# Attention kernel: the next group's filters prepared from step 20 of the last superblock but one, with the spatial filter's products spread among other matmuls

## What is computed

```python
x = x + ddf(gn(x))        # decoupled dynamic filter: 3x3 taps, channel filter times spatial filter
x = x + v * att           # 1x1 products, one sigmoid gate per pixel
x = x + conv3x3(gn(x))    # ternary weights
x = x + attention(gn(x))  # 3136 queries and 3136 keys per image, dk 16, dv 64
```

```python
y  = relu(pooled @ w1.T + b1) @ w2.T + b2            # channel filter, 64 x 9, then centred and scaled
sf = einsum('bchw,nc->bnhw', xn, ws) + bs            # spatial filter, 9 values per pixel
sf = (sf - sf.mean(2)) / (sf.std(2, ddof=1) + 1e-10) # centred and scaled over the 9
```

## Time and profile before

| | us |
|---|---|
| median of 3 runs | 1804.92 |
| lowest and highest | 1804.43, 1806.83 |
| the profiled execution | 1803.89 |
| span of its instructions | 1802.0 |
| TensorE's mean granted clock in it | 0.965 |
| PE, DVE, ACT, POOL busy | 91%, 69%, 67%, 61% of the span |

### The profile page before, as it was taken

How to read it: one execution, slowest core, us unless ns; L and a number is a source line. 1 busy time by engine, 2 the same in 40 slices (tenths; PEclk the granted TensorE clock), 3 DMA queues, 4 the chain that set the end, 5 groups by cost and what they waited for, 6 DMA issues and landing times.

```text
span 1802.0 us, 35669 instructions
## 1 busy us (share of the span) xinstructions
PE 1643.3 (91%) x10892; PEld 835.9 (46%) x10892; DVE 1240.5 (69%) x2443; ACT 1212.8 (67%) x2300; POOL 1101.6 (61%) x926
## 2 busy tenths in 40 slices
PE   5987899999889799999988879999998788999997
PEld 4364444444436345444444634444443364444442
DVE  5946777775584777777367478777738648877760
ACT  2045889998403689999731278999972237899995
POOL 2720488789551058888955106888887402688888
PEclk9989999999989899999988899999999899999999
DMA  2004000000000400000000040000000002000000
GB/s 87 0 1 90 2 7 7 7 7 11 8 0 1 90 2 7 7 7 7 12 8 0 1 90 2 7 7 11 8 7 6 0 20 35 2 12 6 7 7 11
DMA packets 12423, 27.16 MB, mean 15 GB/s; under 512 B 4560, under 2 KB 8912, under 8 KB 11728
## 3 DMA queue, kind: packets, MB, share of 16 engines
q1 hardware_dynamic: 12240, 24.92, 5.9%
HBM read 8.73 MB, written 6.42 MB: 8 GB/s over the span
## 4 chain that ended last, share of the span: by engine, by line
PE 59%; issue 15%; POOL 10%; DVE 9%; ACT 6%; POOLq 1%; DVEq 0%; ACTq 0%
PE PS L1315 26%; PE PS L1271 12%; PE PS L1241 12%; DVE nmt L688 4%; ACT Pb L956 2%; POOL VT L1024 2%; POOL VT L1029 2%; POOL VT L1026 2%; PE PS L1213 2%; DVE nmt L681 2%; POOL VT L1033 2%; ACT PS L911 1%; PE PS L1204 1%; POOL accP L1076 1%; PE PS L1205 1%
## 5 line engine op out<-in xcount | busy, mean ns | idle before, releaser
L681 DVE TENSOR_REDUCE nmt<-PS 128x1 f32<-128x448 f32 x1176 | 681.6, 618 | 211.0 <-PE PS L1241 208.0
L1076 POOL TENSOR_TENSOR accP<-accP,Pb 128x512 f32<-128x512 f32 (+1 forms) x532 | 676.7, 1272 | 125.9 <-ACT Pb L956 97.5
L956 ACT ACTIVATE Pb<-PS 128x896 f32<-128x896 f32 (+1 forms) x700 | 637.5, 915 | 128.5 <-PE PS L1271 118.9
L1315 PE MATMUL PS<-Pb,VT 128*64 128x448 f32 x2800 | 659.9, 544 | 4.8 <-ACT Pb L956 4.1
L1241 PE MATMUL PS<-Ka,Qa 96*64 96x448 bf16 x2888 | 499.8, 358 | 23.6 <-ACT PS L911 10.7
L1271 PE MATMUL PS<-Qa,Ka 99*64 99x448 bf16 x2744 | 491.7, 353 | 3.3 <-ACT Pb L956 2.8
L911 ACT ACTIVATE PS<-PS,nmt 128x448 f32<-128x448 f32 x588 | 356.6, 606 | 30.6 <-DVE nmt L688 28.6
L1241 PEld LDWEIGHTS PS<-Ka,Qa 96*64 96x64 bf16 x2888 | 168.3, 110 | 270.9 <-issue 117.6
L1271 PEld LDWEIGHTS PS<-Qa,Ka 99*64 99x64 bf16 x2744 | 168.4, 110 | 241.8 <-issue 187.4
L1315 PEld LDWEIGHTS PS<-Pb,VT 128*64 128x64 f32 x2800 | 194.9, 137 | 102.6 <-ACT Pb L956 30.3
L834 ACT ACTIVATE xnp<-xw,nb,rstd 128x448 f32<-128x448 f32 x56 | 40.5, 750 | 204.5 <-DVE nb L503 204.5
(11 more groups left out here) (145 smaller groups left out, 1478.4 us busy)
## 6 DMA issues: line engine op xcount, KB each, us to landing
xin<-in_x SPq DMA_DIRECT2D x4, 1568.0 KB, 11.9
out<-xw SPq DMA_DIRECT2D x28, 224.0 KB, 1.9
Qa<-parts SPq DMA_DIRECT2D x24, 168.0 KB, 7.6
Ka<-parts SPq DMA_DIRECT2D x24, 112.0 KB, 3.8
Ka<-parts SPq DMA_DIRECT2D x24, 84.0 KB, 2.6
Qa<-mpt SPq DMA_DIRECT2D x96, 1.3 KB
wz<-in_weights SPq DMA_DIRECT2D x1, 829.0 KB, 8.2
Qa<-parts SPq DMA_DIRECT2D x24, 28.0 KB, 1.9
```

The source lines that it names most:

```text
L681: nc.vector.reduce_max(nmt[:, target % 2, b, t:t + 1], PS[0:BLK, bank, 0:CH], X, negate=True).then_inc(mx_free, 1)
L956: nc.scalar.activation(Pb[0:r, j % PSLOTS, :, :], PS[0:r, 2 * (k % 2):2 * (k % 2) + 2, 0:CH], ACT.Exp).then_inc(exp_done, 1)
L1076: nc.gpsimd.tensor_tensor((accQ if j < TO_ACCP else accP)[0:r, :, REST:CH], (accQ if j <= TO_ACCP else accP)[0:r, :, REST:CH], Pb[0:r, j % ...
L1315: last = mm(PS[C * h:C * h + C, OB, 0:CH], VT[:, j, C * h:C * h + C], Pb[:, j % PSLOTS, h, :], start=(j == 0), stop=(j == NQ - 1))
```

## The change

The preparation keeps its operations and their number. What moves, in steps of superblock 5 and 6 (5/20 is superblock 5, step 20):

| operation | before | after |
|---|---|---|
| DVE `front_stats` | 6/0 | 5/19 (the same place in DVE's order) |
| PE `pair_mean`, `pair_var` | 6/2, 6/3 | 5/20, 5/21 |
| DVE `squares`, `var_eps`, `front_bias` | 6/3, 6/4, 6/6 | 5/20, 5/20, 5/23 |
| POOL `power` | 6/5 | 5/22 |
| ACT `front_normalise` | 6/7 to 6/13 | 5/24, 6/1 to 6/6 |
| PE spatial filter products | 6/8 to 6/14 | 6/2 to 6/8 |
| PE `front_mid` | 6/7 | 6/0 |
| DVE `front_sum_squares` | 6/15 | 6/8 |
| ACT `front_root` | 6/16 | 6/11 |
| PE `front_channel_filter` | 6/16 | 6/12 |
| DVE `front_parts`, `front_centre` | 6/18, 6/19 | 6/12, 6/15 |
| PE transposes | 20, 20, 21, 22, 23, 24, 24 | 16 to 22, one a step |
| POOL `channel_root` | 6/21 | 6/20 |

The four products of a step no longer stand together behind the scores: one stands between the values and the first pair of scores, one between the two pairs, two behind the second pair. The core of the diff:

```diff
-FRONT_XN = 7
-FRONT_SF = 8
-FRONT_TR = (20, 20, 21, 22, 23, 24, 24)
-FRONT_ROOT = 16
+SPLIT_STEP = 17
+FRONT_STATS = SPLIT_STEP + 2
+FRONT_MEAN = 20
+FRONT_XN = (24, 26, 27, 28, 29, 30, 31)
+FRONT_SF = FRONT_XN[0] + 3
+FRONT_SQUARES = 8
+FRONT_ROOT = 11
+FRONT_Y = 12
+FRONT_CENTRE = 15
+FRONT_TR = (16, 17, 18, 19, 20, 21, 22)
+FRONT_CF = 20
...
-            def front_spatial_filter(g, j):
-
-                pe.wait_ge(xn_ready[0], NJ * g + j + 1)
-                for i in range(4 * j, 4 * j + 4):
-                    last = mm(PS[0:SP2, SFB, i * PART:(i + 1) * PART], xnp[:, (2 * i + 1) * PW + 1:(2 * i + 3) * PW + 1],
-                              wcol("ws"), start=True, stop=True)
-                if j == NJ - 1:
+            def filter_rows(g, i):
+
+                if i % 4 == 0:
+                    pe.wait_ge(xn_ready[0], NJ * g + i // 4 + 1)
+                last = mm(PS[0:SP2, SFB, i * PART:(i + 1) * PART], xnp[:, (2 * i + 1) * PW + 1:(2 * i + 3) * PW + 1],
+                          wcol("ws"), start=True, stop=True)
+                if i == NSP - 1:
                     last.then_inc(sfT_ready, 1)
...
-                    if j == 2:
+                    if j == FRONT_MEAN:
                         pair_mean(g + 1, 0, front)
-                    elif j == 3:
+                    elif j == FRONT_MEAN + 1:
                         pair_var(g + 1, 0, front)
-                    elif j == 7:
+                    elif j == NQ:
                         front_mid(g + 1)
-                    elif j == 16:
+                    elif j == NQ + FRONT_Y:
                         pe.wait_ge(recip, NJ * g + NJ)
                         front_channel_filter(g + 1)
...
+                def filter_at(s, j, place):
+
+                    i = NQ * (s - NJ + 2) + j - FRONT_SF
+                    if more and s >= NJ - 2 and 0 <= i < NJ:
+                        for r in ((0,), (1,), (2, 3))[place]:
+                            filter_rows(g + 1, 4 * i + r)
...
                         if j:
                             values(j)
+                        filter_at(s, j, 0)
                         for h in range(2):
                             if j < NQ - 2 or s < NJ - 1:
...
                                 scores(k + 2, s + (j >= NQ - 2), h)
+                            filter_at(s, j, 1 + h)
                             if tiles:
                                 max_tile(*tiles.pop(0))
...
-                        if s == NJ - 1 and more:
-                            front_at(j)
+                        if s >= NJ - 2 and more:
+                            front_at(NQ * (s - NJ + 2) + j)
```

More of the change, by code:

```diff
@@ L937, in front_at @@
                 def front_at(j):
-                    if FRONT_XN <= j < FRONT_XN + NJ:
-                        front_normalise(g + 1, j - FRONT_XN)
-                    for i in range(NJ):
-                        if FRONT_TR[i] == j - 1:
-                            front_spatial_filter(g + 1, i)
-                    if j == FRONT_ROOT:
+                    if j in FRONT_XN:
+                        front_normalise(g + 1, FRONT_XN.index(j))
+                    if j - NQ - 1 in FRONT_TR:
+                        front_spatial_filter(g + 1, FRONT_TR.index(j - NQ - 1))
+                    if j == NQ + FRONT_ROOT:
                         front_root(g + 1)
@@ L982, in group @@
                     superblock(s)
-                if more:
-                    for j in range(NJ):
-                        if FRONT_TR[j] == NQ - 1:
-                            front_spatial_filter(g + 1, j)
                 copy_output(NJ * g + NJ - 1)
@@ L1056, in scale_sums, with superblock @@
                     nc.gpsimd.tensor_tensor(sme[:, :, :], sm[:, s % 2, :, :], ef[:, :, :], ALU.mult).then_inc(dstep, 1)
-                def superblock(sidx, s, first, front=False):
+                def superblock(sidx, s, first):
                     for j in range(1, NQ):
@@ L1061, in superblock @@
                             scale_sums(sidx, s)
-                        if front and j == 5:
+                        if more and s == NJ - 2 and j == FRONT_MEAN + 2:
                             power(g + 1, 0)
-                        if front and j == 21:
+                        if more and s == NJ - 1 and j == FRONT_CF:
                             channel_root(g + 1)
@@ L1084, in group @@
                     superblock(NJ * g + s, s, False)
-                superblock(NJ * g + NJ - 1, NJ - 1, False, more)
+                superblock(NJ * g + NJ - 1, NJ - 1, False)
                 finish(NJ * g + NJ - 1, NJ - 1)
@@ L1288, in front_at @@
                 def front_at(j):
-                    if j == 2:
+                    if j == FRONT_MEAN:
                         pair_mean(g + 1, 0, front)
-                    elif j == 3:
+                    elif j == FRONT_MEAN + 1:
                         pair_var(g + 1, 0, front)
-                    elif j == 7:
+                    elif j == NQ:
                         front_mid(g + 1)
-                    elif j == 16:
+                    elif j == NQ + FRONT_Y:
                         pe.wait_ge(recip, NJ * g + NJ)
                         front_channel_filter(g + 1)
-                    if FRONT_SF <= j < FRONT_SF + NJ:
-                        front_spatial_filter(g + 1, j - FRONT_SF)
-                    for i in range(NJ):
-                        if FRONT_TR[i] == j:
-                            front_transpose(g + 1, i)
+                    if j - NQ in FRONT_TR:
+                        front_transpose(g + 1, FRONT_TR.index(j - NQ))
+                def filter_at(s, j, place):
[3 more added lines that the diff above has]
+                            filter_rows(g + 1, 4 * i + r)
                 def superblock(s):
@@ L1379, in _ @@
             front_mid(0)
-            for j in range(NJ):
-                front_spatial_filter(0, j)
+            for i in range(NSP):
+                filter_rows(0, i)
             front_channel_filter(0)
```

19 lines of the change are left out of this document (8 added, 11 removed).

## The result

The changed kernel takes **1846.07 us** (median of 4 runs, 1845.15 to 1846.84) where the kernel before took 1804.87 on the same chip (1804.43 to 1806.83). The ratio is 1.0224, with a 95% interval of 1.0211 to 1.0237. It is slower, as forecast, but by 41 us and not by 21: the time lies 12 us above the upper end of the range.

A forecast was written before the change was run, and what follows sets the result against it. PE, busy 91% of the span, was taken to bound the kernel. Terms 2.8 + 3.6 + 1.0 = 7.4 us in groups 0 and 2, 6.5 in group 1, total 21.3, gave 1826 us; 8-in-10 range 1806 to 1834.

The forecast's parts named there:

- The mean's wait, 2.80 us: Superblock 5, step 20: PE waits 2.80 us for DVE's statistics ahead of the mean's matmul; +2.8 us a group.
- The spread, 3.6 us a group: Superblock 6, steps 2 to 8: products in three places each pay two switches, 0.51 us more a step; +3.6 us a group.
- B: Rival: spreading the products costs nothing more, as a switch is cheap without a semaphore wait before it; 1815 us, chance 0.20.
- E: Rival: one of each product's two weight loads is hidden; 1807 us, chance 0.10.
- F: Rival: the products' weight loads are all taken ahead and PE's steps fall to POOL's pace; 1799 us, chance 0.07.
- D: Rival: the stall for the mean is absorbed or doesn't occur; 1818 us, chance 0.06.
- the row of one matmul between half-array ones: Trace of the kernel before: a step with one small full-array matmul takes 1.59 us for 1.13, so 0.46 a matmul.
- Root and channel filter, +1.0 us: Superblock 6: +1.8 for the root's wait, -1.7 for the wait for sfp, +0.9 for the transposes; bounds -1 to +2.
- -1.7 for the stall: Ahead of the first transposes in superblock 6: PE's 1.74 us wait for sfp goes, -1.7 us a group.
- The sum without low clock: 2.8 + 3.6 + 1.0 = 7.4 us in groups 0 and 2, 6.5 in group 1; total 21.3 us.
- A: The forecast itself: both the wait for the mean and the products' switches are paid; 1826 us, chance 0.45.
- C: Rival: low clock in addition, three steps at 2.24 for 1.13 us, 7 us in two groups; 1833 us, chance 0.12.

The follow-up runs named there:

- e4: The kernel before with only statistics, mean, variance, var_eps, power and bias moved to the changed kernel's places; 1821.43 us, ratio 1.0083.
- e12: The kernel before with the four products split differently over three places at each of seven steps; steps 2.17 to 2.65 us apart.
- e3: The kernel before with only the four spatial filter products of a step spread one, one and two over three places; 1815.73 us, ratio 1.0055.
- e9: The changed kernel with useless matmuls on PE in both waits, 13 ahead of the mean and 12 in the root's wait; 1825.23 us, ratio 1.0117.
- e15: The kernel before with the first three filter transposes one step later, steps (21, 21, 22, 23, 23, 24, 24); 1804.45 us, ratio 1.0002.
- e2: The changed kernel with 12 useless matmuls on PE in the wait for the root only; 1832.83 us, ratio 1.0158.
- e6: The changed kernel with a step's four products together in one place behind the second half of the scores; 1832.39 us, ratio 1.0165.
- e7: The changed kernel with the channel filter's product y one step earlier, at 6/11 inside the root's gap; 1832.6 us, ratio 1.0155.
- e8: The changed kernel with mean at step 22, a step's products in one place and y at step 11 of superblock 6; 1813.16 us, ratio 1.0045.
- e11: e8 with first normalisation two steps later, squares, root and centring moved by one step, and transposes paired; 1809.59 us, ratio 1.0025.
- e14: e11 with the filters' transposes one to a step, steps 17 to 23, instead of in pairs; 1803.86 us, ratio 0.9996.
- these five kernels: The changed kernel and four versions with useless matmuls filling the mean's wait, the root's, both, or both by half; 1825.23 to 1846.07 us.
- e5: The changed kernel with the mean two steps later, at step 22 of superblock 5, and the variance at step 23; 1838.49 us, ratio 1.0184.

## Why the prediction was right and wrong, step by step

- **The mean's wait, 2.80 us: right.** 2.68 measured, in all groups, in e4 too. Bounds 2.2 to 3.5 held.
- **The spread, 3.6 us a group from steps 2.7 us apart: right.** 2.65 measured, and e12 shows the price by places. That is 3.15 us a group at the steps, a little less than the term; e3's 10.6 us for 10.8 comes so near because a longer wait behind the root is in it. Rivals B, E and F (a cheaper switch, or hidden weight loads) fell with it, as D did with the mean's wait. The choice for the row of one matmul between half-array ones as the nearest price is what carried.
- **Root and channel filter, +1.0 us: right as a sum.** PE waits 2.44 us for 2.5 forecast, L1119 stands behind it, no wait for `sfp`, and the transposes' steps are 1.62 us apart. By subtraction from e9's group 0, 7.0 us longer than before, less 2.68 and 3.15, the part is 1.2. Its piece "-1.7 for the stall" would have been wrong for the kernel before, where e15 shows PE waiting for POOL's last sum instead.
- **The sum without low clock: right.** I forecast 7.4, 6.5 and 7.4 us, 21.3 in all. e9, the changed kernel with nothing but PE's idleness taken away, is 7.0, 6.4 and 7.0 us longer in its three groups and lies 21.7 us above the kernel before (1825.23 for a forecast of 1826).
- **The clock: wrong, and this is the step that failed.** The sum of A put it at nothing; it stood among the rivals, as C, "three steps at 2.24 for 1.13 are 3.3 us; in the two other groups", 7 us in all at a chance of 0.12, and only behind the root. Measured were two stretches in every group, 6.2 us in groups 0 and 2 and 7.6 in group 1, 20 us in all. The row for it stood in the prediction: one stretch, behind a gap that the change was about to make longer. I read it as a matter of chance, because groups 0 and 2 of the kernel before had none, and priced it at that one length; and I asked nothing of the mean's wait, though it was the longest idle of PE that the change would add.
- The range failed for the same reason: it took in the bounds of waits and switches, and only one of the two places of low clock.

That the two waits had such a stretch behind each of them in all three groups is in part the chance of this program's timing: with the mean's wait unchanged, e2, e6 and e7 have five groups of nine without one. The runs don't show what decides it.

What stays open as well: how much of a stretch is the idle itself and how much the small matmuls around it. e2's group 0 and the nine places of e8, e11 and e14 show 3.4 us of low clock behind L1119 with no idle time or 0.34 us of it, so L1119 can count; for the spread's matmuls nothing is shown. That a fill with useful columns would do what useless ones did was not tried.

## What to carry to other kernels

When an edit adds a wait of some microseconds to the engine that bounds the kernel, price it twice: once as time, and once as what the matmuls behind it cost if the granted clock falls. Look in the trace of before for any stretch at 0.50 behind a comparable gap; one occurrence in one group is a warning for all of them, though no promise: put a range on it. In these five kernels a us of low clock cost 0.41 us of time. And follow a wait that is removed down to the next engine: twice here (e5 to ScalarE, e15 to GpSimd) it only changed its place.
